# Reordered start, one ternary rounding on VectorE, later value tables and a last unit in row halves, in a two-layer gated cross-attention kernel

## What is computed

```
x = x + tanh(g_xattn[0]) * xattn0(layernorm(x), ctx)        # 16 heads of 16, softmax over 77 keys
x = x + tanh(g_ffn[0])   * ternary_ffn(layernorm(x))        # 256 -> 1024 -> 256
x = x + tanh(g_xattn[1]) * xattn1(layernorm(x), ctx, dist)  # biases, minus log of distances added to scores
x = x + tanh(g_ffn[1])   * expert(layernorm(x))             # relu 256 -> 1024 -> 256, residual, norm, gamma, beta
```

## Time and profile before

| | us |
|---|---|
| median of 3 runs (lowest, highest) | 415.22 (414.89, 416.18) |
| the profiled execution's own time | 416.79 |
| its span, first to last instruction | 415.0 |
| PE busy | 328.2 (79% of the span) |
| DVE busy | 297.2 (72%) |
| ACT busy | 283.5 (68%) |
| POOL busy | 227.9 (55%) |

### The profile page before, as it was taken

One profiled execution on the slowest core, in us unless ns is written; L12 is line 12 of the kernel. 1 busy time (PEld: TensorE's weight loads), 2 busy tenths in 40 slices (PEclk: granted clock), 3 DMA queues, 4 the chain that ended last, 5 costly groups with the idle time before them and its releaser, 6 DMA issues.

```text
span 415.0 us, 8997 instructions
## 1 busy us (share of the span) xinstructions
PE 328.2 (79%) x3254; PEld 267.5 (64%) x3254; DVE 297.2 (72%) x690; ACT 283.5 (68%) x516; POOL 227.9 (55%) x408
## 2 busy tenths in 40 slices
PE   3658859787876765877787899898878899999990
PEld 2437648566664443455565788687667799888880
DVE  6685747877886657989986467777856558777775
ACT  4137787899896777988953788866678755555520
POOL 5246555776577411456766655567774155544442
PEclk9695898999899869869998999999999999999997
DMA  8996303111100000310073112211100000000001
GB/s 247 243 165 190 77 26 81 38 40 41 42 3 20 2 0 2 52 23 2 2 227 75 49 51 51 51 37 30 37 2 2 2 2 26 28 28 27 25 27 51
DMA packets 23171, 22.02 MB, mean 53 GB/s; under 512 B 4695, under 2 KB 22488, under 8 KB 23051
## 3 DMA queue, kind: packets, MB, share of 16 engines
q1 hardware_dynamic: 23128, 21.45, 20.9%
HBM read 10.34 MB, written 2.10 MB: 30 GB/s over the span
## 4 chain that ended last, share of the span: by engine, by line
PE 38%; DVE 26%; ACT 16%; issue 9%; POOL 8%; DMA 1%; SPq 0%; ACTq 0%; DVEq 0%; POOLq 0%
PE psA L1681 9%; PE psD L1666 4%; PE psBE L1666 4%; DVE st L865 4%; ACT pp_hi L713 3%; POOL lns L399 3%; DVE ham L1155 3%; PE psD L1370 3%; DVE mx L1109 3%; PE psA L1463 2%; ACT p L704 2%; PE psBE L1396 2%; PE psA L1634 2%; POOL pp_lo L491 1%; DVE o L1094 1%
## 5 line engine op out<-in xcount | busy, mean ns | idle before, releaser
L491 POOL TENSOR_TENSOR pp_lo<-p,pp_hi 124x512 f16<-124x512 f32 x80 | 92.7, 1178 | 45.6 <-ACT pp_hi L713 45.6
L399 POOL TENSOR_TENSOR lns<-lns,mhalf 128x2 f32<-128x2 f32 x40 | 32.2, 805 | 117.0 <-DVE lns L870 116.8
L1109 DVE TENSOR_REDUCE mx<-psBE 128x6 f32<-128x462 f32 (+1 forms) x96 | 54.6, 582 | 31.1 <-PE psBE L1396 30.8
L704 ACT ACTIVATE p<-psD 124x512 f32<-124x512 f32 x80 | 47.6, 597 | 28.7 <-PE psD L1370 26.1
L1370 PE MATMUL psD<-qb,ktb 98*124 98x256 f16 (+1 forms) x256 | 50.1, 293 | 5.7 <-DMA qb<-mT 4.8
L713 ACT ACTIVATE pp_hi<-p 124x512 f16<-124x512 f32 x80 | 50.4, 629 | 0.0
L1370 PEld LDWEIGHTS psD<-qb,ktb 98*124 98x124 f16 (+1 forms) x256 | 33.5, 147 | 10.5 <-DMA qb<-mT 6.8
L1396 PE MATMUL psBE<-kt_hi,q_hi 128*128 128x154 f16 (+2 forms) x160 | 34.2, 283 | 5.0 <-ACT mT L695 3.8
L1681 PE MATMUL psA<-ew_lo,pp_hi 128*128 128x256 f16 x128 | 34.9, 273 | 0.0
L1681 PE MATMUL psA<-ew_hi,pp_lo 128*128 128x256 f16 x128 | 34.9, 273 | 0.0
L1681 PE MATMUL psA<-ew_hi,pp_hi 128*128 128x256 f16 x128 | 34.9, 273 | 0.0
(11 more groups left out here) (201 smaller groups left out, 1013.1 us busy)
## 6 DMA issues: line engine op xcount, KB each, us to landing
qb<-q_hi SPq DMA_DIRECT2D x32, 128.0 KB
xs<-in_x SPq DMA_DIRECT2D x8, 256.0 KB, 4.6
tw_raw<-in_tw SPq DMA_DIRECT2D x2, 1024.0 KB, 11.7
qb<-q_lo SPq DMA_DIRECT2D x16, 128.0 KB
space<-in_ew SPq DMA_DIRECT2D x2, 1024.0 KB, 6.5
out<-space SPq DMA_DIRECT2D x8, 256.0 KB, 2.1
ktb<-km SPq DMA_DIRECT2D x6, 248.0 KB, 9.4
qb<-bT_lo SPq DMA_DIRECT2D x8, 104.0 KB
```

Of the source, the lines that this page charges most:

```text
L399: nc.gpsimd.tensor_tensor(lns[:, n % 4, 1, :], lns[:, n % 4, 0, :], mhalf[:, :], ALU.pow).then_inc(s_rs, 1)
L491: nc.gpsimd.tensor_tensor(pl[:, u % 2, 2 * r:2 * r + 2, :], p32[:, n % 4, :, :], ph[:, u % 2, 2 * r:2 * r + 2, :], ALU.subtract).then_inc( ...
L704: a_(p32[:, n % 4, :, :], psD[n % 2][0:KR, :].rearrange("p (t r) -> p t r", t=2), ACT.Exp, scale=1.0 / SSC).then_inc(a["exp"], 1)
L1109: v.tensor_reduce(pairs[:, MP[k][0]:MP[k][1]:MP[k][2], :], psBE[:, n % 2, 0:hn * KEYS].rearrange("p (q e k) -> p q e k", e=2, k=KEYS), AX. ...
```

## The change

1. **Start, order.** DVE makes its two masks before the first statistics; both first units are normalised before `split_keys`; `split_keys` is cut in two (`keys_masked` makes `km`), with two `keys_high` calls put ahead of `keys_masked`; the other two move into attention slots 2 and 3. Statistics of unit 2 and `queries_lo(0, 0)` move ahead of slot 0. PE makes the queries of unit 0 before it transposes unit 1. ACT makes the weight copy for the queries before the keys. SP issues seven loads of row constants ahead of `key_blocks(0)`.
2. **Ternary stage.** The rounding of half j = 1 is a DVE instruction, with a semaphore `q1b`; ACT keeps half 0.
3. **Tables of layer 1.** Value tables in slots 7 to 10 instead of 4 to 7, key tables after slots 3, 4, 9, 10 instead of 3 to 6. The constant column of `vo` (L931) is no longer written again for layer 1.
4. **Last unit.** Its output matmul goes to two banks, by row halves; sum, statistics, factors, norm and store are done by halves.

```diff
@@ SP @@
-            key_blocks(0)
             for o, name in ((bc[:, 0:2], "g_xattn"), ...
                 sp.dma_start(o, io[name].to_broadcast([128, o.shape[1]])).then_inc(d_row, 16)
+            key_blocks(0)
             query_blocks(0, 0)
...
+            u = NU - 1
+            for j in (0, 1):
+                sp.wait_ge(E["out"], u + 1 + j)
+                sp.dma_start(io["out"][u * UR + j * 128:u * UR + (j + 1) * 128, :], y32[:, 1, j, :]).then_inc(d_out[1], 16)
@@ POOL @@
+            def factors_half(j):
+                n = 5 * NU - 1
+                g = lns[:, n % 4, :, j:j + 1]
+                pool.wait_ge(s_var, n + 1 + j)
...
-                factors_dve(4 * NU + u, E["fac"])
+                if u < NU - 1:
+                    factors_dve(4 * NU + u, E["fac"])
+            for j in (0, 1):
+                factors_half(j)
@@ ACT @@
             keys_spread(0)
-            tables_k(0)
             act.wait_ge(d_w[0, "q"], 16)
             a_(spreaded(wqp), spread(wraw[0, "q"]), ACT.Copy).then_inc(s_wqp, 1)
+            tables_k(0)
             ln0_transposed(0)
-            ln0_transposed(1)
...
-                            act.wait_ge(f["q1"], 2 * u)
+                            act.wait_ge(f["q1"], u)
+                            act.wait_ge(f["q1b"], u)
                         a_(h32[:, j, :], hps(n), ACT.Gelu, scale=dq1[:, n:n + 1]).then_inc(f["gelu"], 1)
...
-                    for j in (0, 1):
-                        n = 2 * u + j
-                        act.wait_ge(f["amax"], u + 1)
-                        ge(act, f["phT"], n - 3)
-                        a_(hq[u % 2][:, j, :], h32[:, j, :], ACT.Identity, scale=ham[:, 2, j:j + 1],
-                           bias=epsc[:, 4:5]).then_inc(f["q1"], 1)
+                    act.wait_ge(f["amax"], u + 1)
+                    ge(act, f["phT"], 2 * u - 3)
+                    a_(hq[u % 2][:, 0, :], h32[:, 0, :], ACT.Identity, scale=ham[:, 2, 0:1],
+                       bias=epsc[:, 4:5]).then_inc(f["q1"], 1)
...
             queries_hi(0, 0)
+            ln0_transposed(1)
             tables_v(0)
@@ DVE @@
+            dve.wait_ge(s_const, C_ID)
+            link(v.tensor_reduce(hmask...)); link(v.tensor_reduce(pmask...))     # moved up
             ln0_stats(0)
             ln0_stats(1)
             ln0_apply(0, refine(0, SX))
+            ln0_apply(1, refine(1, SX))
             split_keys(0)
-            ln0_apply(1, refine(1, SX))
-            for i in range(4):
+            for i in range(2):
                 keys_high(0, i)
+            keys_masked(0)
+            ln0_stats(2)
...
+                if (s, r) in ((2, 3), (3, 4)):
+                    keys_high(0, s)
...
                     v.reciprocal(g[:, 2, :], g[:, 1, :]).then_inc(f["amax"], 1)
+                    dve.wait_ge(f["amax"], u + 1)
+                    ge(dve, f["phT"], 2 * u - 2)
+                    v.tensor_scalar(hq[u % 2][:, 1, :], h32[:, 1, :], g[:, 2, 1:2], MAGICQ, ALU.mult, ALU.add).then_inc(f["q1b"], 1)
...
-                if 4 <= s < 8:
-                    if s == 4:
+                if 7 <= s < 11:
+                    if s == 7:
                         dve.wait_ge(A[0]["ppv"], 2 * NU)
-                    tables_v(1, s - 3)
+                    tables_v(1, s - 6)
...
-            for u in (NU - 2, NU - 1):
-                expert_sum(u)
-                expert_norm(u)
+            expert_sum(NU - 2)
+            expert_sum_half(0)      # waits e["half"] and e["xb"] of the last unit; 128x256 sum, bn_stats, bn_aggr, add
+            expert_norm(NU - 2)
+            expert_sum_half(1)      # waits e["pm2"]
+            for j in (0, 1):
+                expert_norm_half(j) # waits e["fac"] of its half
@@ PE @@
                 if l == 1:
                     pe.wait_ge(A[0]["xTh"], NU)
-                    ge(pe, F["xTl"], k)
+                    ge(pe, F["xTl"], k + 3)
...
             ln0_transposes(0)
-            ln0_transposes(1)
...
-                        pe.wait_ge(f["q1"], n + 1)
+                        pe.wait_ge((f["q1"], f["q1b"])[j], u + 1)
...
-                if 4 <= s < 8:
-                    tables_vo(1, s - 4)
+                if 7 <= s < 11:
+                    tables_vo(1, s - 7)
                 ternary_transposed(s - 1)
...
-                    if u < 4:
-                        pe.wait_ge(s_vo, 8 + 2 * u + 1)
+                    if 3 <= u < 7:
+                        pe.wait_ge(s_vo, 8 + 2 * (u - 3) + 1)
...
             before(0, 0)
             queries(0, 0)
+            ln0_transposes(1)
             tables_v(0)
```

More of the change, by code:

```diff
@@ L256, in build @@
              for l in (0, 1)]
-        F = Stage("f0", "pm1 phT pm2 pxT gelu amax q1 hTc res xn xb xTh xTl")
-        E = Stage("f1", "pm1 pm2 relu hlo y fac xgb xb out")
+        F = Stage("f0", "pm1 phT pm2 pxT gelu amax q1 q1b hTc res xn xb xTh xTl")
+        E = Stage("f1", "half pm1 pm2 relu hlo y fac xgb xb out")
         L0 = Stage("l0", "fac xn pxT xT")
@@ L373, in _ @@
                 shift_rows(1, u)
-            for u in range(NU):
+            for u in range(NU - 1):
                 sp.wait_ge(E["out"], u + 1)
@@ L377, in _ @@
                              y32[:, u % 2, :, :]).then_inc(d_out[u % 2], 16)
-            for i in (0, 1):
-                sp.wait_ge(d_out[i], 16 * NU // 2)
+            u = NU - 1
+            for j in (0, 1):
+                sp.wait_ge(E["out"], u + 1 + j)
+                sp.dma_start(io["out"][u * UR + j * 128:u * UR + (j + 1) * 128, :], y32[:, 1, j, :]).then_inc(d_out[1], 16)
+            sp.wait_ge(d_out[0], 16 * NU // 2)
+            sp.wait_ge(d_out[1], 16 * (NU // 2 + 1))
         @block.gpsimd
@@ L426, in factors_dve @@
                 nc.gpsimd.tensor_tensor(g[:, 5, :], g[:, 4, :], g[:, 1, :], ALU.mult).then_inc(done, 1)
+            def factors_half(j):
+                n = 5 * NU - 1
+                g = lns[:, n % 4, :, j:j + 1]
+                pool.wait_ge(s_var, n + 1 + j)
+                nc.gpsimd.tensor_tensor(g[:, 1, :], g[:, 0, :], mhalf[:, 0:1], ALU.pow).then_inc(s_rs, 1)
+                pool.wait_ge(s_rs, n + 1 + j)
+                link(nc.gpsimd.tensor_tensor(g[:, 2, :], g[:, 1, :], g[:, 1, :], ALU.mult))
+                link(nc.gpsimd.tensor_tensor(g[:, 3, :], g[:, 0, :], g[:, 2, :], ALU.mult))
+                link(nc.gpsimd.tensor_scalar(g[:, 4, :], g[:, 3, :], -0.5, 1.5, ALU.mult, ALU.add))
+                nc.gpsimd.tensor_tensor(g[:, 5, :], g[:, 4, :], g[:, 1, :], ALU.mult).then_inc(E["fac"], 1)
             def normalise(n, out, u, scale):
@@ L929, in tables_v @@
                                         vm[:, :, :].unsqueeze(3).to_broadcast([KR, TPH, SLOTS, HD]), ALU.mult)
-                i.then_inc(s_vo, 1)
-                v.tensor_scalar(vo[:, b, hf, :, :, HD], vm[:, :, :], SM * SONE, None, ALU.mult).then_inc(s_vo, 1)
+                i.then_inc(s_vo, 1 + l)
+                if l == 0:
+                    v.tensor_scalar(vo[:, b, hf, :, :, HD], vm[:, :, :], SM * SONE, None, ALU.mult).then_inc(s_vo, 1)
             def ln0_stats(u):
@@ L1210, in expert_sum, with expert_sum_half, expert_norm_half @@
                 stats(4 * NU + u, y, EPS * SY * SY)
+            def expert_sum_half(j):
+                e, u = E, NU - 1
+                n = 4 * NU + u
+                y = y32[:, u % 2, j, :]
+                if j == 0:
+                    dve.wait_ge(e["half"], 1)
+                    dve.wait_ge(e["xb"], u + 1)
+                    dve.wait_ge(d_out[u % 2], 16 * (u // 2))
+                else:
+                    dve.wait_ge(e["pm2"], u + 1)
+                acc = acc_(u)[:, 0:D] if j == 0 else psX[:, D:2 * D]
+                link(v.scalar_tensor_tensor(y, xnk[:, 2 * u + j, :], SY / SX, acc, ALU.mult, ALU.add))
+                link(v.bn_stats(st[:, n % 4, j, :], y))
+                link(v.bn_aggr(mv[:, n % 4, j, :], st[:, n % 4, j, :]))
+                v.tensor_scalar(lns[:, n % 4, 0, j:j + 1], mv[:, n % 4, j, 1:2], EPS * SY * SY, None,
+                                ALU.add).then_inc(s_var, 1)
+            def expert_norm_half(j):
+                e, u = E, NU - 1
+                n = 4 * NU + u
+                y = y32[:, u % 2, j, :]
+                dve.wait_ge(e["fac"], u + 1 + j)
+                link(v.scalar_tensor_tensor(y, y, mv[:, n % 4, j, 0:1], gg[:, :], ALU.subtract, ALU.mult))
+                dve.wait_ge(e["xgb"], u + 1)
+                v.scalar_tensor_tensor(y, y, lns[:, n % 4, 5, j:j + 1], xgb[:, u % 2, j, :],
+                                       ALU.mult, ALU.add).then_inc(e["out"], 1)
             def expert_norm(u):
@@ L1239, in _ @@
                 ternary_slot(s)
-                if s < 7:
-                    keys_high(1, s - 3)
+                if s == 4:
+                    keys_high(1, 1)
             queries_lo(1, 0)
@@ L1244, in _ @@
             ternary_slot(NU + 1)
+            keys_high(1, 2)
             attn_slot(1, 1, 3 * NU)
             ternary_slot(NU + 2)
```

(10 more changed lines are left out.)

17 lines of the change are left out of this document (9 added, 8 removed).

## The result

| | before | changed |
|---|---|---|
| median (lowest, highest), us | 415.06 (414.37, 416.18), 4 runs | 422.22 (419.97, 422.67), 4 runs |
| profiled execution, its span | 416.79, 415.0 | 422.67, 420.9 |
| ratio, 95% interval | | 1.0159, 1.0116 to 1.0202 |

The change makes the kernel 7.2 us slower by the medians (6.6 by the ratio, which is taken over the means); forecast were 2.7 us, and 422.22 lies outside the range that was given. The sign was right, the size was not. Between the two profiled executions the difference is 5.9 us.

What follows compares the result with a forecast made beforehand. No engine alone was taken to bound the kernel (PE 38%, DVE 26%, ACT 16% of the wait chain). Terms -3.8 + 0.15 - 0.13 + 6.3 + 0.2 gave +2.7 us: median 417.9, 8-in-10 range 412.3 to 420.3.

Steps and rivals of the forecast that it cites:

- Start, -3.8: Start: earlier norms, queries and maxima, then scores limited by the DMA backlog at about 30.2 instead of 33.18; -3.8 us.
- -2.5: Start: the bound of least gain, -2.5 us, if the blocks land a little later still.
- +0.15: Ternary slots 3 to 7: five roundings +7.2 us against table work and a wait removed; sum +0.15 us.
- -0.13: Ternary slots 0 to 2: ACT's saved rounding gains almost nothing; DVE's slot 3 starts at 172.35 instead of 172.48.
- R: Slots 3 to 7: average time of each new DVE rounding with its wait for POOL, 1.44 us, bounds 0.75 and 2.0.
- Slot 8, +2.95: Slot 8: PE's table waits for DVE's last psX read, holding transposes and output matmul; residual of unit 6 2.95 us late.
- rival C: Tables slower than said and PE's clock falling in its new waits: +2 us on top, 420; chance 0.14.
- Slots 9 and 10, +3.35: Slots 9 and 10: PE's and DVE's tables delay output matmul and maxima, +1.3 us in slot 9, +2.05 in slot 10.
- Tail, +0.2: Last unit: DVE's half sum waits for POOL's L531, +0.3 us; last store half as large, -0.1; I take +0.2.
- A: Key blocks land in time at the start and slots 9, 10 are half hidden: -2.0 us, 413.2, faster; chance 0.17.
- B: Rounding in slots 3 to 7 seldom meets POOL, R = 0.75: 3.4 us less, 414.5, just within no change; chance 0.14.
- D: Slots 8 to 10 cost what is said and the start gives 5.7 us: 416.0, no change; chance 0.15.

Runs made afterwards that it cites:

- the start alone: The kernel before with only the new order of the start: ratio 0.9967 (0.9943 to 0.9991), which is -1.4 us.
- the tables alone: The kernel before with only the later layer 1 value and key tables, constant column written in layer 0 alone: ratio 1.0131 (1.0105 to 1.0157), +5.4 us.
- rounding alone: The kernel before with only the second ternary rounding of each unit moved to DVE: ratio 1.0148 (1.0119 to 1.0176), +6.1 us.
- fillers: The changed kernel plus 19 and 10 unused matmuls ahead of PE's value tables of slots 7 and 8: 1.0124 and, again, 1.0118 to the kernel before.
- later loads: New start, column of ones in layer 0 alone, ternary weights and seven rows issued behind shifts: 0.9862; with the distance tables later too, 1.0062.

## Why the prediction was right and wrong, by its steps

**Start, -3.8: too much, and two steps of it failed.** The norms, queries and maxima moved as worked out: maxima at 18.31 on DVE instead of 21.51, inside the 17.2 to 18.2 but for 0.1. The step by which the blocks are last to land and the scores start at about 30.2 found the right resource and the wrong item: the shifts' DMA is last, and PE gets past it anywhere from 30 to 34, behind the same backlog. My -2.5 was meant as the bound for that; the start alone is worth -1.4 (-0.4 to -2.4). The two traces of the changed kernel have -3.0 and -3.9 at the ternary stage, that of the start alone -1.5; why is open. And that the two key tables moved to slots 2 and 3 cost nothing was wrong for slot 2: the wait that hid them was DVE's, but POOL paid (0.58). The Trainium skill ("SBUF — State Buffer", section "Who interferes with whom") has that a VectorE instruction with two SBUF inputs contends with a GpSimd instruction that reads SBUF; the rows at 47.58 and 47.73 agree. I had thought of DVE's waits only.

**Ternary slots 0 to 7: the sum right, in part by luck.** +0.15 forecast, +0.18 measured in slots 3 to 7, -0.10 for -0.13 in slots 0 to 2. The new DVE instruction takes 0.75 in slots 0 to 2, then 1.67, 0.93, 0.92, 1.40, 1.40: R = 1.26 for the 1.44 taken, inside the bounds. Five of them are 6.3 us and not 7.2, so all the other terms together gave 6.1 and not the 7.05 of the sum: two errors of 0.9 that cancel. The 0.75 with POOL idle is right; it came from the slope of the rows. With the tables alone, slots 3 to 7 lose 3.2, where my terms without the rounding give 7.05. A term that is worth its full length because the engine has no gap holds until the next engine, here ACT, has none.

**Slot 8, +2.95: the failing term.** Measured +5.98. The mechanism and every instruction of it were as said: table at DVE's last read, transposes, output matmul, residual. The step that failed is the sum 0.1 + 0.71 + 0.91 + 1.76 = 3.5: its durations were taken from the earlier trace rows, at full clock, and the wait that the step itself creates took that clock away. At half clock the stretch takes 6.53 us; with the clock held, 3.55. This was named as rival C, with 2 us for all its waits and a chance of 0.14; it is what happened, and it needed 3.0 in slot 8 alone. What spoke for it stood in my own rows: queries at 0.45 us a matmul behind a wait of 4.13. For each new wait in the sum I should have priced what follows it at half clock as well.

**Slots 9 and 10, +3.35: right, once the clock is taken out.** Measured +2.6. Slot 9 of the kernel before has a fall of the clock of its own (windows of the kernel before):

```profile
225.00:230.00 5.00, 5.00 (x30) 4.03 (x29) 1.47 (x3) 1.71 (x3) 3.88 (x7) 0.66 0.17 39
```

The changed kernel has it later (its windows):

```profile
235.00:240.00 5.00, 3.30 (x24) 2.73 (x23) 3.27 (x7) 2.22 (x5) 0.80 (x1) 0.81 0.19 55
240.00:245.00 5.00, 5.00 (x39) 4.37 (x38) 2.00 (x5) 3.41 (x7) 4.04 (x4) 0.85 0.22 47
```

So it moved from slot 9 to slot 10. Slot 9 without it is 11.06 (rounding alone), so the table costs 1.24 there (1.3 forecast); slot 10 without it is 11.03 (fillers), +2.2 (2.05 forecast).

**Tail, +0.2: the sum right, its terms not.** 0.2 in the traces, DVE waiting for L547 as said; alone 1.0000, which a run can't tell from +0.2 or from -0.9. The prediction reads DVE's end before as 412.0, the end of the first of two L1222; the second ends at 412.40, and its +0.3 is 412.7 less that. Counted from the shifts of unit 2, DVE's end came 0.6 later (418.71 in the changed kernel), and the time from it to the end of the span fell by 0.4, from 2.6 to 2.2, where -0.1 was said. The two misses cancel.

**Rivals.** A (blocks in time) did not occur with the loads as they are; it is what later loads make of the start. B (rounding seldom meets POOL) did not occur as said: the rounding waited in all five slots, though less than 0.2 us in two of them, and R = 1.26 is nearer to 1.44 than to 0.75. D fell with slot 8. In the profiled pair the sum misses by 3.2: 3.0 in slot 8, 0.8 in the start, less 0.7 in slots 9 and 10. Over the median it misses by 4.5: the profiled execution of before lies 1.7 above its median, that of the changed kernel 0.4 above its own. Over medians the start counts for more than the 0.8, since alone it gave -1.4 for -3.8: 2.4 in the start, 3.0 in slot 8, less 0.7 in slots 9 and 10 is an estimate of 4.7 for those 4.5. The fillers fit it: with PE kept at work the kernel is still 5 us slower than before, not 2.7.

**Still open.** Why the shifts' DMA, two of 4 KB issued at 24 to 26 us, let PE start anywhere between 30 and 34; whether that differs by program or by execution; and what decides in which stretch of slots 8 to 10 the clock of PE falls when none of its waits is long.

## What to carry to other kernels

When a step puts a new wait of some us on PE, price the matmuls behind it at half clock as well, then add the wait, and give that case a real chance: here waits of 2.49, 3.52 and 4.79 us had a fall with them, while one of 2.87 us in the changed kernel, at 229 us, had none (granted clock 1.00 from 225 to 235). When a stage starts earlier, ask which DMA is issued last before it and how many bytes stand ahead of that one; take away those that nothing needs yet, after looking up who waits for each. And price work moved into one engine's gap by what its neighbour does in that gap, not by the gap alone.

## What the runs showed of the hardware that was not expected

- PE at half clock behind waits of only 2.49 us (granted clock 0.50 for 208 to 212 us), soon after an earlier fall; useless matmuls in the wait (2.32 us of them) kept it at 1.00.
- 16 matmuls of 128x256 took 1.91 us at full clock and 3.62 at half, 16 transposes 1.05 and 1.88.
- A DVE instruction of 0.79 us with two SBUF inputs held a POOL instruction of two elements a partition from 0.19 to 0.69 us.
- PE's wait for the same DMA of 4 KB was 2.30 and 2.00 us in two executions of the changed kernel, and 4.82 and 3.81 in two of the kernel with fillers, whose start has the same instructions.
